# Six gathered blocks instead of four, and edge groups of 1220 edges instead of 1280, in a graph layer on one core

## The reference

```python
h = jnp.maximum(_layernorm(x, axis=-1), 0.0)
m = h[src] + edge_attr
aggr = jax.ops.segment_sum(m, dst, num_segments=N_NODES)
hidden = jax.nn.relu(aggr @ W1 + b1)
mlp_out = hidden @ W2 + b2
out = x + (1.0 + eps[0]) * h + mlp_out
```

## Time and profile before

| | |
|---|---|
| median of 3 runs | 564.34 us (557.04 to 564.97) |
| the profiled execution | 561.21 us |
| its span in the profile | 559.3 us |
| granted TensorE clock, mean over the span | 0.994 |
| TensorE / VectorE / ScalarE / GpSimd busy | 493.2 / 486.6 / 418.4 / 337.2 us |
| bytes from and to HBM | 112.50 and 6.48 MB |

### The profile page before, as it was taken

How to read it: one execution, slowest core, us unless ns; L and a number is a source line. 1 busy time by engine, 2 the same in 40 slices (tenths; PEclk the granted TensorE clock), 3 DMA queues, 4 the chain that set the end, 5 groups by cost and what they waited for, 6 DMA issues and landing times.

```text
span 559.3 us, 23317 instructions
## 1 busy us (share of the span) xinstructions
PE 493.2 (88%) x9560; PEld 462.1 (83%) x9560; DVE 486.6 (87%) x712; ACT 418.4 (75%) x637; POOL 337.2 (60%) x200
## 2 busy tenths in 40 slices
PE   0436899999989999999999899999998999999995
PEld 0325799999878888889999798899887998999994
DVE  7996999999997978898999789899896889999960
ACT  0798778888776867868888578788774788788771
POOL 1310003888888888888888888888888878000000
PEclk9999999999999999999999999999998999999998
DMA  7689988988889979999989789998876779667000
GB/s 193 237 283 279 273 268 263 280 219 222 206 226 244 268 205 249 246 276 228 241 212 235 169 206 259 300 225 235 219 199 154 207 207 239 187 203 214 16 10 19
DMA packets 99110, 120.58 MB, mean 216 GB/s; under 512 B 71160, under 2 KB 72792, under 8 KB 98870
## 3 DMA queue, kind: packets, MB, share of 16 engines
q1 hardware_dynamic: 74854, 108.13, 64.0%
q0 software_dynamic: 24144, 10.89, 15.1%
HBM read 112.50 MB, written 6.48 MB: 213 GB/s over the span
## 4 chain that ended last, share of the span: by engine, by line
PE 78%; ACT 8%; DVE 7%; issue 5%; DMA 1%; SPq 0%; DVEq 0%; ACTq 0%
PE agg_ps L1021 29%; PE oct_ps L1009 22%; PE agg_ps L1015 16%; PE key_ps L1033 5%; PE mlp_ps L1038 4%; ACT gathered_edges L894 3%; ACT adj L858 2%; DVE lo_hot L561 2%; DVE z L561 2%; PE key_ps L1026 1%; DMA gathered_edges<-in_dst 1%; ACT hid L871 1%; DVE hl L591 0%; DVE hot L568 0%; ACT hl L882 0%
## 5 line engine op out<-in xcount | busy, mean ns | idle before, releaser
L858 ACT ACTIVATE adj<-oct_ps 128x784 f16<-128x784 f32 x360 | 299.0, 865 | 108.6 <-PE oct_ps L1009 90.9
L490 POOL DMA_INDIRECT gathered_edges<-h_rows,gather_src x160 | 301.3, 1883 | 48.8 <-issue 48.8
L1021 PE MATMUL agg_ps<-hl,adj 128*128 128x192 f16 x2205 | 234.1, 246 | 2.0 <-issue 1.5
L561 DVE TENSOR_TENSOR lo_hot<-iota_z,key 128x2048 f16<-128x2048 f16 x180 | 219.3, 1218 | 0.0
L1009 PE MATMUL oct_ps<-z,lo_hot 128*128 128x98 f16 x2880 | 192.4, 209 | 17.7 <-DVE lo_hot L561 6.5
L561 DVE TENSOR_TENSOR z<-z_marks,key 128x1568 f16<-128x1568 f16 x180 | 174.3, 969 | 12.7 <-PE oct_ps L1009 7.0
L1009 PEld LDWEIGHTS oct_ps<-z,lo_hot 128*128 128x128 f16 x2880 | 165.3, 100 | 22.6 <-issue 11.2
L1021 PEld LDWEIGHTS agg_ps<-hl,adj 128*128 128x128 f16 x2205 | 174.2, 98 | 4.9 <-issue 2.9
L1015 PE MATMUL agg_ps<-edges,hot 128*32 128x96 f32 x3600 | 98.8, 252 | 16.4 <-issue 13.9
L1015 PEld LDWEIGHTS agg_ps<-edges,hot 128*32 128x32 f32 x3600 | 81.2, 111 | 29.9 <-issue 20.7
L461 POOL DMA_INDIRECT win<-packed_keys,row_i x23 | 30.3, 1317 | 74.7 <-DMA gathered_edges<-in_edge_attr 61.2
(11 more groups left out here) (126 smaller groups left out, 182.5 us busy)
## 6 DMA issues: line engine op xcount, KB each, us to landing
edges<-in_edge_attr SPq DMA_DIRECT2D x180, 480.0 KB
gathered_edges<-in_edge_attr SPq DMA_DIRECT2D x16, 480.0 KB
dst<-in_dst SPq DMA_DIRECT2D x180, 5.0 KB
gathered_edges<-h_rows,gather_src POOLq DMA_INDIRECT x160
out<-ob SPq DMA_DIRECT2D x45, 48.0 KB
packed_keys<-adj SPq DMA_DIRECT2D x1, 1632.0 KB, 6.8
h_rows<-gathered_edges SPq DMA_DIRECT2D x1, 1200.0 KB, 9.2
h_rows<-gathered_edges SPq DMA_DIRECT2D x1, 1152.0 KB, 9.0
```

Source lines behind the costliest of these rows:

```text
L490: nc.gpsimd.indirect_dma_start(out=gathered[k][:, g, t, :], out_offset=None, in_=h_dram, in_offset=bass.IndirectOffsetOnAxis(ap=gather_src ...
L561: return nc.vector.tensor_tensor(out.rearrange("p t (w two) -> p t w two", two=2), marks[0:out.shape[0], 0:width].rearrange("p (o w two) - ...
L858: return nc.scalar.activation(adj[k][:, :, 2 * OCT * o:2 * OCT * (o + 1)].rearrange("p h (t q) -> p t h q", q=2), oct_ps[:, o % 2, :].rear ...
L1021: last = nc.tensor.matmul(agg_ps[buf][:, 0:2 * C], adj[buf][:, h, :], hl[:, h, :], start=False, stop=(h == NT - 1), skip_group_check=True)
```

## The change

- GATHERED goes from 4 to 6, so the main blocks from 45 to 43; the gathered ones hang on main blocks 10, 16, 22, 28, 34 and 38.
- An edge window is GP = 122 partitions with ten edges each, 1220 edges, in every load, one-hot and edge sum, for main and gathered blocks.
- The gathers fetch rows of 384 bytes that hold both f16 halves of h (the DRAM copy of h is stored from `hl`), without an add, into a buffer of their own. The edge rows of a gathered block come through the same three edge buffers as all others; main and gathered blocks form one sequence of 49 runs (`RUNS`) for the loads.
- TensorE sums a gathered block in two parts: 40 f16 matmuls over the gathered rows (192 columns), 40 f32 matmuls over the edge rows. VectorE makes the one-hot in f16, ScalarE widens it to f32 and scales it, VectorE adds the two halves of the result.
- Indices of dst have six buffers (IDS) and are loaded two runs ahead of the rows; the source indices of all gathered blocks are loaded once, at run 3.
- A key fetch stands before every 12 gathers; `residual` has 6 pieces instead of 9; the last nine of 49 tiles of h are made on VectorE; some early tensors share memory.

```diff
+GP = 122
-GATHERED = 4
-ATTACHED = (14, 24, 34, 42)
+GATHERED = 6
+ATTACHED = (10, 16, 22, 28, 34, 38)
-FETCH_EVERY = 25
-FETCH_PER = 3
+FETCH_ROWS = 12
+IDS = 6
-RES_ROWS = 5
+RES_ROWS = 8
...
-    GE = P * GT
+    GE = GP * GT
-        h_dram = nc.dram_tensor("h_rows", [NT * P, C], F32).ap()
+        h_dram = nc.dram_tensor("h_rows", [NT * P, 2 * C], F16).ap()
...
+            def load_ids(s):
+                if s >= NT:
+                    return
                 for g in range(GROUPS):
...
+                    at = RUNS[s] * GROUPS + g
+                    e0 = sp.value_load(e_tab[0:1, at:at + 1], min_val=0, max_val=ELAST)
+                    sp.dma_start(dst_sb[s % IDS][0:GP, g, :], dst[bass.ds(e0, GE)].rearrange("(p t) -> p t", t=GT)).then_inc(ids_in[s % IDS], 16)
+
+            def load_edges(s):
                 for g in range(GROUPS):
...
+                    at = RUNS[s] * GROUPS + g
                     e0 = sp.value_load(e_tab[0:1, at:at + 1], min_val=0, max_val=ELAST)
...
+                    sp.dma_start(edges[s % TURN][0:GP, g, :, :], edge[bass.ds(e0, GE), :].rearrange("(p t) c -> p t c", t=GT)).then_inc(edges_in[s % TURN], 16)
...
+            for s in range(TURN, NT):
+                sp.wait_ge(edges_done, s - TURN + 1)
+                load_edges(s)
+                load_ids(s + 2)
+                if s == TURN:
+                    load_sources()
+                    store_h(0)
+                    store_h(1)
...
+            pool.wait_ge(gather_src_in, 16 * GATHERED * GROUPS)
             pool.wait_ge(h_stored, 32)
             for j in range(GATHERED):
                 k = gathered_buffer(j)
-                pool.wait_ge(gather_in[k], (j // 2 + 1) * (2 * 16 * GROUPS))
+                if j < 2:
+                    pool.wait_ge(res_ready, 1 if j == 0 else len(RES))
+                else:
+                    pool.wait_ge(edges_done, runs_until(NM + j - 2))
                 for g in range(GROUPS):
                     for t in range(GT):
...
                         nc.gpsimd.indirect_dma_start(
-                            out=gathered[k][:, g, t, :], out_offset=None, in_=h_dram,
-                            in_offset=bass.IndirectOffsetOnAxis(ap=gather_src[k][:, g, t:t + 1], axis=0),
-                            compute_op=ALU.add).then_inc(gather_done[k], 16)
...
+                            out=gather_rows[k][0:GP, g, t, :], out_offset=None, in_=h_dram,
+                            in_offset=bass.IndirectOffsetOnAxis(ap=gather_src[0:GP, j, g, t:t + 1], axis=0)).then_inc(gather_done[k], 16)
...
+                        s = run_of(b)
+                        pe.wait_ge(edges_in[s % TURN], (s // TURN + 1) * (16 * GROUPS))
+                        sum_edges(edge_rows(b), hot[b % 2], agg_ps[b % 2][:, 0:C], True).then_inc(edges_done, 1)
+                        if here is not None:
+                            k, s = gathered_buffer(here), run_of(NM + here)
+                            pe.wait_ge(gather_narrow, here + 1)
+                            pe.wait_ge(gather_done[k], (here // 2 + 1) * (16 * GROUPS * GT))
+                            sum_gathered_rows(gather_rows[k], gather_hot16, agg_ps[b % 2][:, 2 * C:4 * C])
+                            pe.wait_ge(gather_wide, here + 1)
+                            pe.wait_ge(edges_in[s % TURN], (s // TURN + 1) * (16 * GROUPS))
+                            sum_edges(edge_rows(NM + here), gather_hot, agg_ps[b % 2][:, 2 * C:3 * C], False).then_inc(edges_done, 1)
```

More of the change, by code:

```diff
@@ L109, in build @@
         rel16 = sb("rel16", [P, GROUPS, GT, 2], F16)
-        rel = [sb(f"rel{k}", [P, GROUPS, GT]) for k in range(2)]
+        rel = sb("rel", [P, GROUPS, GT])
         key2 = [sb(f"key{k}", [P, 2, 2 * TPB, 2], F16) for k in range(2)]
@@ L247, in build @@
         edges_in = [sem(f"edges_in{k}") for k in range(TURN)]
-        ids_in = [sem(f"ids_in{k}") for k in range(TURN)]
+        ids_in = [sem(f"ids_in{k}") for k in range(IDS)]
         rel_ready = sem("rel_ready")
@@ L316, in attached, with run_of, runs_until @@
             return ATTACHED.index(b) if b in ATTACHED else None
+        RUNS = []
+        for b in range(NM):
+            RUNS.append(b)
+            if b in ATTACHED:
+                RUNS.append(NM + ATTACHED.index(b))
+        def run_of(b):
+            return RUNS.index(b)
+        def runs_until(b):
+            return RUNS.index(b) + 1
         def gathered_buffer(j):
@@ L321, in edge_rows @@
         def edge_rows(b):
-            return edges[b % TURN]
+            return edges[run_of(b) % TURN]
         block = ctx.enter_context(nc.Block())
@@ new lines, in load_sources, with store_h @@
+            def load_sources():
+                for j in range(GATHERED):
+                    for g in range(GROUPS):
+                        at = (NM + j) * GROUPS + g
+                        e0 = sp.value_load(e_tab[0:1, at:at + 1], min_val=0, max_val=ELAST)
+                        sp.dma_start(gather_src[0:GP, j, g, :], src[bass.ds(e0, GE)].rearrange("(p t) -> p t", t=GT)).then_inc(gather_src_in, 16)
+            def store_h(k):
+                t0, t1 = ROWS[k].start, ROWS[k].stop
+                sp.wait_ge(hl_ready, k + 1)
+                sp.dma_start(h_dram[t0 * P:t1 * P, :].rearrange("(t p) c -> p t c", p=P), hl[:, t0:t1, :]).then_inc(h_stored, 16)
@@ L375, in _ @@
             sp.wait_ge(tab_ready, 1)
[L376 to L396, removed]
+            load_ids(0)
+            load_edges(0)
+            load_ids(1)
+            load_edges(1)
+            load_ids(2)
+            load_edges(2)
+            load_ids(3)
+            load_ids(4)
+            for s in range(TURN, NT):
[6 more added lines that the diff above has]
+                    store_h(1)
+                if RUNS[s] >= NM:
+                    continue
+                b = RUNS[s]
                 if b >= STORE_LAG:
@@ L586, in normal, with rest_of_h @@
                                                ALU.mult, ALU.mult).then_inc(norm_ready, 1)
+            def rest_of_h():
+                v.wait_ge(norm_ready, 3)
+                for t in range(SCALAR_H, NT):
+                    last = nc.vector.tensor_scalar(h_sb[:, t, :], x_sb[:, t, :], rstd[:, t:t + 1], shift[:, t:t + 1], ALU.mult, ALU.add)
+                chain(last)
+                nc.vector.tensor_scalar(h_sb[:, SCALAR_H:NT, :], h_sb[:, SCALAR_H:NT, :], 0.0, None, ALU.max).then_inc(h_rest, 1)
             def low_part(k):
                 v.wait_ge(h_ready, k + 1)
+                if k == 1:
+                    v.wait_ge(h_rest, 1)
                 v.wait_ge(high_ready, k + 1)
@@ L753, in _ @@
                 chunk(b, 0)
+                if attached(b - 1) is not None:
+                    join_gathered(attached(b - 1))
                 if b == 0:
                     normal(2)
-                if b == 1:
+                    rest_of_h()
+                    first_hots()
+                if b == 2:
                     keep_sorted()
@@ L887, in _ @@
             nc.scalar.activation(steps.bitcast(F32), steps, ACT.Relu, scale=-1.0, accum_out=falls[:, 0:1]).then_inc(falls_ready, 1)
-            for t in range(NT):
+            for t in range(SCALAR_H):
                 if t in DEVIATION_AT:
@@ L1014, in sum_edges, with sum_gathered_rows @@
                     for g in range(GROUPS):
-                        last = nc.tensor.matmul(sums[GROUP * g:GROUP * (g + 1), :], hots[:, g * GT + t, :], rows[:, g, t, :],
+                        last = nc.tensor.matmul(sums[GROUP * g:GROUP * (g + 1), :], hots[0:GP, g * GT + t, :], rows[0:GP, g, t, :],
                                                 start=fresh and t == 0, stop=False, skip_group_check=True)
                 return last
+            def sum_gathered_rows(rows, hots, sums):
+                for t in range(GT):
+                    for g in range(GROUPS):
+                        nc.tensor.matmul(sums[GROUP * g:GROUP * (g + 1), :], hots[0:GP, g * GT + t, :], rows[0:GP, g, t, :],
+                                         start=False, stop=False, skip_group_check=True)
             def sum_slots(buf, h0, h1):
```

186 lines of the change are left out of this document (96 added, 90 removed).

## The result

The changed kernel takes 2165.17 us (median of 4 runs, 2163.95 to 2165.49) where the kernel before took 563.73 us beside it: a ratio of 3.878, with an interval of 3.860 to 3.896. The forecast was 2130. The profiled execution has a span of 2162.1 us.

The account below looks back on a forecast made before the run. TensorE bounds the kernel before; after the change, 122-row loads on two DMA engines do. 1970 + 18 + 70 + 25 + 27 + 22 = 2132 us of span, 2 us around it; predicted 2130 us, range 1870 to 2500.

Parts of the forecast that it names:

- The step that decided: Edge loads: row count sets the number of DMA engines; 122 is 2 x 61, so two engines instead of 16.
- Always the same pair: SP queue: all 122-row transfers fall on the same two engines and form one line, 40.2 us a block.
- The price of a row: Edge loads: 147 ns for a 3840 B row, plus 350 ns an engine and transfer; 9.3 us a load.
- the prediction's upper rule: Plain queue: packet time less non-edge packets at 19 ns, over the edge rows; it gave 191 ns a row.
- The upper price, 191 ns: Edge row price from above, laid to sixteen engines in each other's way; not used for two engines.
- The sum: Whole span: 1970 us for 49 blocks, 18 sources, 70 gathers, 25 stores, 27 start, 22 tail: 2132 us.
- the first rival: GpSimd's 122-row gathers use the same pair, adding 320 to 830 us: 2380 to 2890 us; 6%.
- The second and third: Rivals with transfers spread over engines: TensorE decides, 541 to 566 us, 8%; or GpSimd bounds, 702 us, 4%.
- Its sign doesn't matter here: TensorE and GpSimd balance, hidden under the transfers; net on TensorE -8.4 us, from -8 to +6.
- the second rival: 122-row transfers spread out, edge rows come in time and TensorE decides: 541 to 566 us; 8%.
- Its TensorE term: TensorE: two converted blocks save 14 us, six f16 sums at 0.95 us add 5.7 us; net -8.4 us.
- The signs: Changed profile: DMA share 0.13 to 0.2, 50 to 60 GB/s, 40 us blocks, TensorE idle 30 us, lower clock.

Follow-up runs that it names:

- 61 + 61 kernel: Changed kernel with its 122 rows, each edge load cut into two transfers of 61 and 61 rows; 3906.09 us (one run).
- the first experiment: Changed kernel with only the row count set back from 122 to 128; 604.33 us, ratio 1.110 to the kernel before.
- four kernels: Changed kernel at 128 rows: sources spread, dst loaded with edges, five or four gathered blocks (754.5, 743.95 us); or edge loads cut 112 + 16, 64 + 64 (853.11, 886.91 us).

## Why the prediction was right, step by step

**How many engines.** The step that decided held: 106 and 126 rows in the trace of before gave the rule, and in the runs one, two and four engines showed it by share and by block, sixteen by the time: 604 us.

**Always the same pair.** Taken, not shown, in the prediction. The 61 + 61 kernel shows it for one engine. For the pair there is the changed kernel itself: its queue was full and q1 still had 2.1 engines.

**The price of a row.** 147 ns and 350 ns for the first is 153 ns a row. The changed kernel's q1, by the prediction's upper rule: 0.134 x 16 x 2162.1 = 4635 us, less 43774 others at 19 ns, over 23912 edge rows: 159 ns at most. The upper price, 191 ns, was rightly left to sixteen engines.

**The sum.** First edge load at 31.8 us (27.4 taken), last edge sum at 2138.8, 23.3 us ahead of the end (22 taken). Between them 49 runs of 43.0 us. The forecast had 40.2 us and, spread over the 49, the sources, stores and sixteenth of the gathers, 113 us or 2.3 a block: 42.5. The 30 us between 2132 and 2162 are 49 x 0.5, 4.5 and 1.3. Two terms can hold the 49 x 0.5: q0's 4.3% of 16 engines is 93 us an engine, if it is spread evenly, where 70 were taken for the gathers, and a row may have cost up to 159 ns instead of 153. The 25 us for stores had no working beside them; they are a hundredth of the sum.

**Gathers elsewhere.** 0.27 against 0.13 in the windows, and no block over 50 us in the timeline shown: the first rival is out. The second and third, spread transfers, are out with a DMA slice of 1.

**What lay hidden.** "Its sign doesn't matter here" was true, and it hid two sums of mine that were wrong. A gather of 122 rows costs 1703 + 300 ns, not 1.6 us; I had taken over the price of a fetch of 128. (A gather of 128 rows did cost about that, 1352 + 300 ns.) And the second rival's 541 to 566 us would not have come even with sixteen engines: 604 us. Its TensorE term was right (0.95 us taken and 1.01 found for the f16 sum), but it lacked SP: 24 source loads in a row, which hold back edge rows and the start of the gathers (the first at 109.8 us, where I had some 80), and perhaps eight loads a block that leave SP no pause. The 8 us that TensorE was to win showed in no time. They do show in its work: TensorE was busy 479.7 us in the first experiment, against 493.2, but it waited 48.4 us for gathers and 26.5 for edge rows.

**The signs.** DMA share, bytes per second, TensorE's idle time and the lower clock came as named. The chain was to go through edges and DMA; it names SP's issue for 91% instead. A full queue shows itself as the length of the issuing instruction, not as a wait for the transfer.

## What to carry to other kernels

Before a tile size changes the row count of a transfer, take the largest divisor of that count up to 16. In SP's queue here it was the number of DMA engines at work (one, two and four of them in these runs), and since they were the same ones each time, transfers behind each other didn't fill the rest. Short lone transfers at the start and end of a trace show the rule at no cost, as engines times 1/16 in the share of a narrow window. And where one bound is four times the others, a sum that it hides is untested: set the bound aside in a run of its own before the rest of the change is called good.

## What the hardware showed that was not expected

- A load with its read of the start took SP 0.9 to 1.1 us in the 128-row kernels; the issuing instruction alone has a median of 0.33 us. In front of a full queue that instruction took 8.6 us.
- GpSimd's gather has the transfers' trait too: 1703 ns and 27936 packets in q0 at 122 rows, 1423 ns and 16416 at 124, 1352 ns and 8736 packets at 128, for 240 gathers and 22 fetches each. With an add in it, 160 gathers of 122 rows made 159824 packets; with 128 rows the queue had 24144.
- 120 rows, fifteen engines by the rule, cost 248 ns a row and 128 rows on sixteen 178. Not explained.
- In four kernels TensorE, VectorE and ScalarE paused for microseconds without a releaser, and these kernels were 1.33 to 1.58 times as long as the kernel before. Not explained; all four ran on one chip.
